# Graph convolutions on one core: conv 2's residual is made one pair ahead on ScalarE instead of two

## The reference

```
h  = relu(layernorm(x))
# block 1, residual around it
r  = h                                # "residual": relu(layernorm(x))
h  = gelu(layernorm(gcn(h, W1, b1)) * g1 + be1)      # conv 1
h  = layernorm(gcn(h, W2, b2)) * g2 + be2            # conv 2
x  = x + gelu(h + r)                                 # -> x2
# block 2
h  = relu(layernorm(x))
x  = x + gcn(h, W3, b3)                              # conv 3
```

## Time and profile before

| | |
|---|---|
| median of 3 runs | 3254.38 us (3251.54 to 3256.09) |
| time of the profiled execution | 3252.1 us |
| its span, first to last instruction | 3250.3 us |
| busy over the span: PE, PEld, DVE, ACT, POOL | 90%, 75%, 79%, 61%, 64% |
| mean granted TensorE clock | 0.991 of full speed |
| conv 2, first to last instruction of `residual` | about 1341 us to 2350 us of the span |

### The profile page before, as it was taken

One profiled execution on the slowest core, in us unless ns is written; L12 is line 12 of the kernel. 1 busy time (PEld: TensorE's weight loads), 2 busy tenths in 40 slices (PEclk: granted clock), 3 DMA queues, 4 the chain that ended last, 5 costly groups with the idle time before them and its releaser, 6 DMA issues. The chain is left out here.

```text
span 3250.3 us, 61089 instructions
## 1 busy us (share of the span) xinstructions
PE 2915.3 (90%) x16547; PEld 2447.4 (75%) x16547; DVE 2560.4 (79%) x6385; ACT 1986.2 (61%) x2965; POOL 2074.8 (64%) x1619
## 2 busy tenths in 40 slices
PE   8223359999999999799999999999869999999999
PEld 2122248888888888688888888888758888888888
DVE  9899968888888888699999999999934544544444
ACT  0256547777776777588888888888833333333333
POOL 0122257777777776588888888888755555555553
PEclk9999999999999999899999999999989999999999
DMA  3499987788888886699999999999789999999996
GB/s 130 158 359 418 416 251 215 213 217 218 214 217 216 217 215 173 221 323 327 329 321 332 322 329 328 325 328 325 271 241 284 288 290 290 285 289 286 287 287 209
DMA packets 306304, 890.91 MB, mean 274 GB/s; under 512 B 67591, under 2 KB 69033, under 8 KB 306248
## 3 DMA queue, kind: packets, MB, share of 16 engines
q1 hardware_dynamic: 190408, 682.26, 59.3%
q0 software_dynamic: 115840, 208.01, 28.1%
HBM read 653.10 MB, written 308.07 MB: 296 GB/s over the span
## 5 line engine op out<-in xcount | busy, mean ns | idle before, releaser
L889 POOL DMA_INDIRECT gathered<-H,idx x826 | 1153.7, 1397 | 518.5 <-issue 240.6
L1278 PE MATMUL out<-Whi,ahi 128*128 128x512 f32 x2832 | 774.8, 395 | 9.4 <-ACT out L972 9.3
L1278 PE MATMUL out<-Wlo,ahi 128*128 128x512 f32 x2832 | 760.5, 390 | 0.0
L963 ACT ACTIVATE ahi<-agg 128x1024 fp32r<-128x1024 f32 x354 | 360.9, 1019 | 641.5 <-PE agg L1269 641.5
L1278 PE MATMUL out<-Whi,alo 128*128 128x512 f32 x2832 | 739.2, 390 | 0.1
L1278 PEld LDWEIGHTS out<-Wlo,ahi 128*128 128x128 f32 x2832 | 532.9, 188 | 115.5
L1278 PEld LDWEIGHTS out<-Whi,alo 128*128 128x128 f32 x2832 | 531.5, 188 | 110.8 <-DVE alo L1089 0.5
L1278 PEld LDWEIGHTS out<-Whi,ahi 128*128 128x128 f32 x2832 | 511.9, 189 | 114.5 <-ACT out L972 20.1
L1081 DVE TENSOR_TENSOR vlo<-gathered,vhi 128x512 fp32r<-128x512 f32 x354 | 242.8, 686 | 318.1 <-ACT vhi L957 318.1
L1089 DVE TENSOR_TENSOR alo<-agg,ahi 128x1024 fp32r<-128x1024 f32 x354 | 428.8, 1211 | 33.6 <-ACT ahi L963 33.1
L1255 PE MATMUL agg<-ident,gathered 128*128 128x128 f32 x2832 | 369.9, 274 | 57.5 <-DMA gathered<-H,idx 46.7
(11 more groups left out here) (176 smaller groups left out, 3827.2 us busy)
## 6 DMA issues: line engine op xcount, KB each, us to landing
gathered<-H SPq DMA_DIRECT2D x351, 512.0 KB, 6.1
H<-ho SPq DMA_DIRECT2D x250, 512.0 KB, 4.2
x<-in_x_dram SPq DMA_DIRECT2D x165, 512.0 KB, 7.5
X<-x SPq DMA_DIRECT2D x117, 512.0 KB
x<-X SPq DMA_DIRECT2D x117, 512.0 KB, 7.5
out_dram<-conv SPq DMA_DIRECT2D x117, 512.0 KB
H<-x SPq DMA_DIRECT2D x48, 512.0 KB, 9.8
gathered<-H,idx POOLq DMA_INDIRECT x826, 6.1
```

What stands on the lines that cost most here:

```text
L889: pool.indirect_dma_start(rows, None, H[q][0:end, :], bass.IndirectOffsetOnAxis(ap=idx[p.slot(4)][:, c:c + 1], axis=0), bounds_check=end - ...
L963: nc.scalar.activation(Ahi[p.slot(2)][:, :], Agg[p.slot(2)][:, :], ACT.Copy)\
L1278: m = nc.tensor.matmul(Out[2 * p.slot(2) + j][:, :], a[p.slot(2)][:, c:c + P], w[q][:, f, :], start=False, stop=stop and f == KD - 1, skip ...
```

## The change

In conv 2, ScalarE's body p now makes the residual of pair p+1 where it made that of pair p+2, at the same place in the body. Ahead of the first body it makes that of pair 0 alone, where it made those of pairs 0 and 1. Nothing else is changed: the same instructions, buffers, waits and DMAs stand in the kernel, and no other engine's order changes.

```
                             if second:
                                 high(p.after(1))
                                 over_high(p.after(2))
-                                for k in range(2):
-                                    relu_x(k, p.after(k))
+                                relu_x(0, p)
                                 over_high(p.after(3))
                                 seed(1, p.after(1))
...
                             if has(known, -2):
                                 relu_x2(of(known, -2), p.after(-2))
-                            if has(known, 2):
-                                relu_x(of(known, 2), p.after(2))
+                            if has(known, 1):
+                                relu_x(of(known, 1), p.after(1))
                             if has(known, 4):
                                 over_high(p.after(4))
                             return
```

## The result

| | before | changed |
|---|---|---|
| median of the timed runs | 3252.96 us | 3510.42 us |
| ratio to before, 95% interval | | 1.0789 (1.0768 to 1.0811) |
| span of the profiled execution | 3250.3 us | 3507.2 us |
| forecast | | 3468 us (3436 to 3550) |

Three of the four runs behind the 3510.42 us took 3509.0 to 3510.9 us (median 3509.9) at a mean granted clock of 0.972, and the fourth took 5713.4 us at 0.869, which the ratio leaves out.

The account below looks back on a forecast made before the run. TensorE sets the pace at 8.61 us a pair, VectorE close behind; a 10.48 us ring replaces it: +209 us over 112 pairs, +4 for the last three, +1 at the start, +214 together, giving 3468 us (3436 to 3550).

Parts of the forecast that it names:

- The wait for x: ScalarE's 94.0 us before L1003 in conv 2; claimed to cost the kernel only of the order of 9 us.
- The residual comes about 6 us too late: In conv 2, L1003 ends 7.9 us later in ScalarE's order against 2.0 us of cover, so GpSimd waits.
- The ring of one pair: Conv 2 dependency loop from gelu through L1003, L925, gather, power and VectorE to the next gelu; chance 0.82.
- The length of the ring: Sum of the loop's steps on VectorE, ScalarE and GpSimd with hand-overs: 10.48 us a pair, against TensorE's 8.6.
- The upper bound: Slower hand-over to GpSimd (0.28 us) and a 1.47 us gather: 11.09 us a pair, about 3537 us.
- the low end: Lowest bound, with VectorE's part 1.54 us and hand-over 0.03: 10.25 us a pair, about 3442 us.
- The port: Rival: GpSimd's L925 and VectorE's L1147 exclude each other; if GpSimd loses, 3545 to 3625 us; chance 0.09.
- TensorE's clock still 1.00: Sign: TensorE's granted clock in conv 2 stays at 1.00 although it stands still about 2 us a pair.
- The signs: Conv 2: L925 10.3 to 11.1 us apart, GpSimd waiting for L1003, VectorE for L932, TensorE busy 8.5 of 10.5.
- The gain: Rival: GpSimd's queue does not bind, so TensorE's 9.3 us behind the seed go: about 3245 us; chance 0.03.
- the hidden wait: Rival: GpSimd has 6 us of slack in the body, so the time stays at 3254 us; chance 0.02.
- the clock at the lower level for good: Rival: TensorE at the 1.2 GHz level, up to 17 us a pair, some 4200 us; chance 0.03.

Follow-up runs that it names:

- e7: Kernel before, with SyncE's load of x moved ahead of its two other loads in the body: 3243.5 us, ratio 0.9972.
- e12: Changed kernel, with ScalarE's L1003 of the next pair at the front of the body, ahead of squares: 3246.3 us, ratio 0.9980 to the kernel before.
- e4: Changed kernel, with VectorE's x2_sum (L1146) reading x alone, leaving out the addition of the gelu: 3471.2 us, ratio 1.0673 to the kernel before.
- e11: Changed kernel, with GpSimd's gather behind power and x2_sum reading x alone: 3356.1 us, ratio 1.0315 to the kernel before.
- e1: Changed kernel, with GpSimd's power ahead of the pair's residual and of the gather: 3472.8 us, ratio 1.0680 to the kernel before.
- e3: Changed kernel, with ScalarE's L1003 of the next pair ahead of L1022 instead of behind it: 3425.5 us, ratio 1.0534 to the kernel before.
- e9: Changed kernel, with power ahead of the residual and x2_sum reading x alone: 3335.0 us, ratio 1.0254 to the kernel before.
- e2: Changed kernel, with GpSimd's gather behind power instead of ahead of it, the residual still first: 3435.5 us, ratio 1.0566 to the kernel before.
- e6: Kernel before, residual still made two pairs ahead, with only GpSimd's power put ahead of the residual: 3473.4 us, ratio 1.0679.
- e5: Changed kernel, with L1003 ahead of L1022 and GpSimd's power ahead of the gather: 3412.3 us, ratio 1.0485 to the kernel before.

## Why the prediction was right, and what was off

- *The wait for x is worth about 9 us and not 94.* Right. e7 takes it away by itself: 9 us.
- *The residual comes about 6 us too late and GpSimd waits.* Right; 3.1 us of waiting a pair in the longer pair. e12 shows that the place behind gelu is what does it, not "one pair ahead".
- *The ring of one pair with GpSimd's queue in it.* Right, step by step in the timeline. In all 83 turns looked at gelu begins behind L1134. e4 against e11 shows the gather as a member of the ring. That power is one is shown by VectorE's 150.0 us before L1167, and by their end in e1.
- *The length of the ring, 10.48 us.* Low by 0.35 to 0.39. The term that was mis-sized is "GpSimd from the start of the first L925 to the end of L932: 4.78 us": it took 5.08, since the gather took 1.34 us beside L1146 and not 1.03. The upper bound had this in it (1.47 us); I stayed near the low end with the reason that the gather "took 1.03 us in all 104 cases". All 104 stood beside L1120 and its small neighbours, with one large operand in SBUF at most, and the change moved the gather to another. The sisters behind power, whose 1.47 us the upper bound used, stood beside L1147, L1135 and L1081, which read two. The hand-over to VectorE was 0.16, not 0.03; the rest is within 0.05.
- *The port.* The rival was put as GpSimd losing. In the changed kernel it is mostly VectorE that is held (L1146 1093 ns; L925 stays at 1291 ns), and it had room: VectorE still waits 1.3 us a pair for power. So the time is the ring's. The forecast had said that nothing changes if VectorE loses; that was wrong by the 0.3 us of the gather. It also said that no row shows such a pair at 512 columns, which is so; but L1162, on two columns, took 415 ns beside L925, and that was a sign of it. The Trainium skill, "SBUF — State Buffer", section "Who interferes with whom", calls the port pair that VectorE and GpSimd share an exclusive lock, and says that issue order and not the shape decides who is blocked; the rows agree, with instructions on two columns that last 1259 (e3) and 1112 ns (e9) beside an L925 of 1292 and 1283. In e1 both sides lengthen, L1146 to 1742 and L925 to 1507 ns: as if each waited for the other in turn.
- *What I did not see.* Behind the ring stood a second limit of nearly the same height. The numbers expected of e1, e2 and e3 were worked out from the ring alone, and the three took 74 to 200 us more than that. e6 settled it: the kernel before pays 220 us for L925 beside L1147, with no part of the change in it.
- *TensorE's clock still 1.00.* Wrong: 0.94 in conv 2, without a price that shows.
- *The signs.* The residuals are 10.87 us apart, GpSimd's wait is for L1003, L932 stands behind the gather. But L1147's counterpart took 1.09 us where more than 0.7 was named as a sign of being wrong, VectorE waits 1.3 us for power and not 2, and TensorE is busy 9.2 of 10.9 us and not 8.5 of 10.5. The first two go with the held VectorE, the third with the lower clock, at which its work takes longer.
- *The rivals.* The gain, the hidden wait and the clock at the lower level for good did not come.

What stays open is how a VectorE instruction lengthens a gather, and by how much. L889 took 0.99 to 1.04 us in every run (1400 to 2300 us) wherever no 512-column instruction with two operands in SBUF ran beside it, and 1.06 to 1.58 us where one ran beside it for 0.5 us or more. e4 shows that the operands matter at the same place. But the gather behind power took 1.06 us beside L1134 in the changed kernel, and the first gather 1.53 us beside the same line in e9, and no run shows what makes that difference.

## What to carry to other kernels

When work is moved later on an engine, follow what it releases round until you come back to the same instruction of the next turn; the number of turns that the ring spans divides its length, and going from two to one here made 5.2 us a pair (worked out) into 10.8 (measured). Count every instruction that stands between in an in-order queue, such as `power`, which needed nothing of the residual. Then ask what each moved instruction of GpSimd now stands beside on VectorE: an instruction's time in the old trace holds only for its old neighbour.

## What the runs showed of the hardware that was not expected

- A GpSimd tensor_tensor on 128x512 float32 (1.29 us) holds even a VectorE instruction on two columns, if that reads two operands from SBUF: 137 to 161 ns became 960 to 1284 ns (e3, e5, e9). Instructions with one operand in SBUF, or with theirs in PSUM, kept their times beside it: L1146 with one operand took 676 to 678 ns (e4, e9).
- A gather issued by GpSimd (indirect DMA) took 0.99 to 1.04 us with no 512-column VectorE instruction of two SBUF operands beside it, and 1.06 to 1.58 us with one: 1.34 on the mean beside L1146 (changed kernel), 1.55 (e5), 1.53 beside L1134, which has no running sum (e9).
- TensorE's granted clock fell to 0.50 behind a gap of 2.13 us in the changed kernel, while other gaps of the same length there, and gaps of 3.2 us in the preparation, left it at 1.00.
